# Reordering three ScalarE steps and two VectorE steps in the first two token pairs of a four-layer conditional residual kernel

## The chip, the cores and the metric

The kernel runs on one core of a Trainium2 chip. The metric is the device time of one execution in microseconds; the number given for a kernel is the median of its runs. A profile is one further execution, recorded by the hardware profiler. The core's engines are called PE (TensorE), ACT (ScalarE), DVE (VectorE), POOL (GpSimd) and SP (SyncE, which issues most transfers here). PSUM is the memory that PE writes, SBUF the one from which all engines read.

## The reference

Four residual layers are applied one after the other to x (32 sequences of 64 tokens, 1024 features), all in float32:

```
x = x + W0[adapter[b]] applied across the 64 tokens of sequence b
x = x + x @ W1 + (x @ A1[adapter[b]]) @ B1[adapter[b]]
x = x + x @ W2.T + 0.5 * (x @ A2[labeler[b]]) @ B2.T
logits = x @ Wr.T + 5.0 * onehot(language[b]);   top 2 of 8, softmax -> gates
x = x + x @ W3.T + 2 * sum over experts e of gates[e] * (x @ A3[e].T) @ B3[e].T
```

## The kernel before

**Folding.** The three wide layers are linear up to the low-rank terms, so the kernel multiplies the weight matrices (I + W1)(I + W2)(I + W3) into one 1024 x 1024 matrix first; this takes about the first 245 us of the profile. Then it runs over the tokens, 128 (two sequences, a "block") at a time. Two blocks make a pair; there are eight pairs.

**Two-part numbers.** Every matmul operand is kept as a high part (ACT or POOL writes it, rounded) and a low part (the value minus the high part, mostly on DVE). A product takes three matmuls: high x high, low x high, high x low. Making the two parts of an operand is called splitting it: `..._hi` on ACT, `..._lo` on DVE.

**Seven products.** The product of a pair of blocks with the folded matrix is a Strassen-Winograd product of 2 x 2 quarters: seven products p1 to p7 in place of eight, with sums of the left quarters (made on POOL, in `first_sum` and `pair_sums`) and four combinations t1 to t4 of the right quarters b11, b12, b21 and b22. The combinations are formed once, on DVE (`front_sum`, `back_sum`), and split once (`combination_hi` on ACT, `split_lo` on DVE). Each has a front of three rows of blocks, 128 x 1536 elements in memory, and a back of one row, 128 x 512. The first pair (`first_pair_products`) uses the plain eight quarter products, so that the combinations are needed only from the second pair on, where the calls `there("t1")` to `there("t4")` in `pair_products(1, ...)` wait for the low parts.

**A block's chain.** `narrow` multiplies the block with the 232 narrow columns (low-rank matrices, router). `xn_hi` and `xn_lo` split the result, `mixed` applies the layer-0 matrix. DVE copies the first low-rank activations to `h1c` (`first_low_rank`), PE transposes them (`h1_across`), ACT copies the transpose to `h1T` (`h1_t`), PE multiplies (`h1_into`). The same follows for the second layer with `h2c` (`second_low_rank`), `h2_across`, `h2T` (`h2_t`) and `h2_into`. Then come `route` (the top 2), `exp_of` on ACT, `gates` (which ends in `gh`), and `gated_across`, PE's transpose of `gh`. Then four output tiles are multiplied (`tile`). PE's order has these small steps written in by hand between parts of the wide products.

**What sets the order.** Each engine executes one list of instructions, written out by hand, with semaphore waits; an instruction that waits holds up everything behind it on its engine. The first pair has its own lists (`first_pair_hi` on ACT, `first_pair_lo` on DVE). The second pair is `pair_hi(1, ...)` and `pair_lo(1, ..., after_first=True)`, whose extra lines split t2 and t4. The third-layer low-rank matrix b3 is loaded by SP (line 555) and split on ACT and DVE; it is needed for the first output tile.

In the second pair b0 is block 2 and b1 is block 3. In the rows, line 1165 is the one helper for every `..._lo`, line 1365 is `back_sum`, line 1370 `front_sum`, line 1077 b3's split on ACT, line 879 the ACT copy of a back row, line 1028 `h2_t`, line 1004 the split of a left operand, line 1036 `exp_of`, line 1548 the last step of `gates`, line 1566 `sum_p7`, lines 1510 and 1515 `second_low_rank`. On PE line 1932 is a wide product of the first pair, line 1869 one of the other pairs, line 1896 `h2_across`, line 1901 `h2_into`, line 1885 `h1_across`, line 1906 `gated_across`. On POOL line 697 is `first_sum`, line 681 the last left sum of a row pair of the folding stage, line 643 the low part of the layer-0 matrix.

Of the kernel before, what the change touches and what calls it, by code (L numbers as in the profile page):

```python
# [35 lines left out]
def cond_resid_kernel(nc, x, idx_adapter, idx_labeler, idx_language, w0, w1, a1, w2, a2, b2, w3, b3, out):  # L36
# [59 lines left out]
    def at(name, shape, dtype, offset):  # L96
        return nc.alloc_sbuf_tensor_at(name, shape, dtype, offset=offset)

    def pair(name, shape, offset):
        size = 4  # L100
        for n in shape[1:]:
# [31 lines left out]
                  t4=[W2S[z][:, 0:KQ, BANK:BANK + F3C] for z in range(2)])  # L133
# [35 lines left out]
    def low_back(name):  # L169
# [5 lines left out]
              t3=at("t3_hi", [P, KH, BANK], F32R, X0 + 5 * HALF), t4=M12[0])  # L175
# [94 lines left out]
    with ExitStack() as ctx:  # L270
# [126 lines left out]
        FRONT, BACK = "f", "b"  # L397
# [347 lines left out]
        def _(act):  # L745
# [127 lines left out]
            def split_hi(name, part):  # L873

                dst = m_operand(name, 0) if name[0] == "b" else TH[name]
                if part == FRONT:
                    nc.scalar.activation(dst[:, 0:KF, :], raw_front(name), ACT.Copy).then_inc(s_mh, 1)
                else:
                    nc.scalar.activation(dst[:, KF, :], raw_back(name), ACT.Copy).then_inc(s_mh, 1)

            def combination_hi(name, part):
                act.wait_ge(s_tf if part == FRONT else s_tb, FORMED[name])
                split_hi(name, part)

            def plain_hi(dst, src):
                nc.scalar.activation(dst, src, ACT.Copy).then_inc(s_ph, 1)
# [27 lines left out]
            def row_out(j, name, src):  # L914
                nc.scalar.activation(m_row(j, name), src[:, :], ACT.Copy).then_inc(s_ra, 1)
# [100 lines left out]
            def xn_hi(b, to):  # L1016

                act.wait_ge(s_nar, b + 1)
                above(act, s_small, 3 * b - 2)
                nc.scalar.activation(XN[0], quarters(bank[to][:, 0:SC]), ACT.Copy).then_inc(s_xnh, 1)  # L1020

            def h1_t(b, s):
                act.wait_ge(s_th, 2 * b + 1)
                nc.scalar.activation(h1T[s][:, :], bank[RT + s][0:2 * SEG1, Z1], ACT.Copy).then_inc(s_hts, 1)

            def h2_t(b, s):
                act.wait_ge(s_th, 2 * b + 2)
                nc.scalar.activation(h2T[s][:, :], bank[RT + s][0:SEG2, Z2], ACT.Copy).then_inc(s_hts, 1)
# [9 lines left out]
            def xm_hi(slot, src):  # L1038
                nc.scalar.activation(XM[slot][0], src[:, :], ACT.Copy).then_inc(s_xmh, 1)
# [13 lines left out]
            def first_pair_hi():  # L1053

                for j in range(NR):
                    rows_pair_hi(j)
                act.wait_ge(s_radd, 3 * (NR - 1))
                split_hi("b22", FRONT)
                act.wait_ge(s_ra, 2 * NR)
                split_hi("b12", BACK)  # L1060
                act.wait_ge(s_rw, PRODUCTS * NR)
                row_out(LASTR, "b21", bank[BB])
                act.wait_ge(s_ra, 2 * NR + 1)
                split_hi("b21", BACK)
                act.wait_ge(s_radd, 3 * NR)
                split_hi("b22", BACK)
                act.wait_ge(s_raw[1], 16 * (NR + 2))
                plain_hi(CS[0], raw[1][:, 0:KH, :])
                plain_hi(DS[0], raw[1][:, KH:K, :])
                combination_hi("t3", FRONT)  # L1070
                combination_hi("t1", FRONT)
                combination_hi("t1", BACK)
                xn_hi(0, YB)
                combination_hi("t2", FRONT)
                h1_t(0, 0)
                act.wait_ge(s_b3, 16)
                nc.scalar.activation(B3[0][:, :], b3raw[:, :], ACT.Copy).then_inc(s_b3h, 1)
                combination_hi("t3", BACK)
                h2_t(0, 0)
                left_hi(1)  # L1080
                exp_of(0)
                combination_hi("t2", BACK)
                xn_hi(1, YB)
                act.wait_ge(s_nar, 2)
                act.wait_ge(s_pw, 3)
                xm_hi(0, bank[BA])
                h1_t(1, 1)
                xm_hi(1, bank[BB])
                ght_hi(0, 0)
                h2_t(1, 1)  # L1090
                combination_hi("t4", FRONT)
                combination_hi("t4", BACK)
                exp_of(1)
                xn_hi(2, YB + 1)
                act.wait_ge(s_pw, 5)
                act.wait_ge(s_mix, 1)
                xm_hi(0, bank[BD_])
                ost_even(0, 0)
                ght_hi(1, 1)
                act.wait_ge(s_mix, 2)  # L1100
                xm_hi(1, bank[BC])
                first_ost_odd(1)
                ost_even(0, 2)
                first_ost_odd(3)
# [56 lines left out]
        def _(dve):  # L1161
# [214 lines left out]
            def split_lo(name, part):  # L1376

                dst = m_operand(name, 0) if name[0] == "b" else TH[name]
                dve.wait_ge(s_mh, SPLIT_HI[name + part])
                if part == FRONT:  # L1380
                    out_ = m_operand(name, 1)[:, 0:KF, :] if name[0] == "b" else low_front(name)
                    lo(out_, raw_front(name), dst[:, 0:KF, :], s_ml)
                else:
                    out_ = m_operand(name, 1)[:, KF, :] if name[0] == "b" else low_back(name)
                    lo(out_, raw_back(name), dst[:, KF, :], s_ml)
# [88 lines left out]
            def ght_lo(b, s):  # L1474
                dve.wait_ge(s_ghh, b + 1)
                lo(GHT[s][1][:, :], bank[RT + s][:, Z1], GHT[s][0][:, :], s_ghl)
# [16 lines left out]
            def first_low_rank(b, s, steps):  # L1493
                nar = bank[RT + s]
                dve.wait_ge(s_small, 3 * b + 1)
                for h in range(PER):
                    ts, at_ = slice(h * T, (h + 1) * T), C3 + PER * R2 + h * R1
                    steps.then(V.tensor_copy(h1c[ts, h * SEG1:h * SEG1 + 2 * R1].rearrange("p (m r) -> p m r", m=2),
                                             nar[ts, at_:at_ + R1].unsqueeze(1).to_broadcast([T, 2, R1])))
                steps.hold()  # L1500
                for h in range(PER):
                    ts, at_ = slice(h * T, (h + 1) * T), C3 + PER * R2 + h * R1
                    lo(h1c[ts, h * SEG1 + 2 * R1:(h + 1) * SEG1], nar[ts, at_:at_ + R1], h1c[ts, h * SEG1:h * SEG1 + R1], s_h1c)
# [122 lines left out]
            def pair_lo(p, last, steps, after_first=False):  # L1626
                b0, b1 = 2 * p, 2 * p + 1
                ops = OPS * p - OPS

                operand_lo(CS[1], tmp[:, :, :], CS[0], ops + 2)  # L1630
                first_low_rank(b0, 0, steps)
                if after_first:
                    dve.wait_ge(s_tf, FORMED["t4"])
                    split_lo("t2", FRONT)
                    dve.wait_ge(s_tb, FORMED["t4"])
                    split_lo("t2", BACK)
                operand_lo(DS[1], tmp[:, :, :], DS[0], ops + 3)
                second_low_rank(b0, 0, steps)
                operand_lo(XB[1][:, :, :], raw[1][:, :, :], XB[0][:, :, :], ops + 4)
                route(b0, 0, steps)  # L1640
                if after_first:
                    split_lo("t4", FRONT)
                    split_lo("t4", BACK)
                    xn_lo(b1, YB)
                sum_p1(p)
                operand_lo(CS[1], raw[1][:, 0:KH, :], CS[0], ops + 5)
                sum_p5(p)
                if not after_first:
                    xn_lo(b1, YB)
                gates(b0, 0, steps)  # L1650
                operand_lo(XB[1][:, 0:KH, :], tmp[:, :, :], XB[0][:, 0:KH, :], ops + 6)
                first_low_rank(b1, 1, steps)
                ght_lo(b0, 0)
                sum_p7(p)
                second_low_rank(b1, 1, steps)
                xm_lo(0, bank[BA], 4 * p + 1)
                if not last:
                    left_lo(p + 1)
                route(b1, 1, steps)
                xm_lo(1, bank[BD_], 4 * p + 2)  # L1660
                gates(b1, 1, steps)
                if not last:
                    xn_lo(b0 + 2, YB + 1)
                ght_lo(b1, 1)
                xm_lo(0, bank[BC], 4 * p + 3)
                xm_lo(1, bank[BB], 4 * p + 4)
                ost_odd(p, 1)
                ost_odd(p, 3)
# [467 lines left out]
```

## Time and profile before

| what | value |
|---|---|
| time, median of 3 runs | 523.62 us (523.47 to 523.71) |
| the profiled execution | 525.11 us, of which the span is 523.1 us |
| PE busy | 515.4 us (99%) |
| PEld (weight load, overlaps PE) busy | 449.3 us (86%) |
| DVE busy | 333.1 us (64%) |
| ACT busy | 201.1 us (38%) |
| POOL busy | 169.2 us (32%) |
| granted TensorE clock | full in all of the span |

The span is the time from the first to the last recorded instruction; the rest of the profiled execution lies around it. Busy time counts instructions that run, not those that wait. Times in rows are microseconds from the start of the span.

### The profile page before, as it was taken

The numbers are of one execution on the slowest core, as the hardware profiler recorded it, in microseconds if no ns is written. First come the engines' busy times: TensorE is split into PE (matmuls) and PEld (weight loads), VectorE is DVE, ScalarE is ACT, GpSimd is POOL, SyncE is SP. The second block draws the span as 40 slices with busy tenths as digits, with TensorE's granted clock in tenths as the row PEclk, the third lists the DMA queues.
The fourth block names the chain that finished last, engine by engine and source line by source line (L and its number), as shares of the span: only waits on it lengthen the run. The fifth ranks groups of instructions, "written<-read, shape, count | busy, mean of one in ns | idle before, by whom it ended". The sixth has DMA issues, their size and how long they took to land.

```text
span 523.1 us, 8849 instructions
## 1 busy us (share of the span) xinstructions
PE 515.4 (99%) x2716; PEld 449.3 (86%) x2716; DVE 333.1 (64%) x654; ACT 201.1 (38%) x349; POOL 169.2 (32%) x250
## 2 busy tenths in 40 slices
PE   7999999999999999999999999999999999999997
PEld 7999999988988888888788788888888888888885
DVE  3798797699533333399776864756647557476464
ACT  5644652345132222267344333323332333333322
POOL 2540000002102020219546434444254434553400
PEclk9999999999999999999999999999999999999999
DMA  8911310213430202040703303313233032222312
GB/s 262 375 60 27 72 40 1 80 41 122 154 116 0 81 0 81 0 166 3 241 1 117 121 12 123 104 41 113 83 115 120 37 113 85 75 84 77 125 28 80
DMA packets 29343, 46.80 MB, mean 89 GB/s; under 512 B 12020, under 2 KB 17396, under 8 KB 29188
## 3 DMA queue, kind: packets, MB, share of 16 engines
q1 hardware_dynamic: 29124, 45.85, 26.8%
q0 software_dynamic: 192, 0.59, 0.3%
q8 instruction: 16, 0.26, 0.2%
q14 instruction: 11, 0.09, 0.1%
HBM read 33.39 MB, written 13.04 MB: 89 GB/s over the span
## 4 chain that ended last, share of the span: by engine, by line
PE 91%; DMA 2%; POOL 1%; issue 1%; SPq 1%; DVE 1%; POOLq 1%; ACT 1%; ACTq 0%; DVEq 0%
PE bank L1869 25%; PE bank L1803 13%; PE bank L1735 11%; PE bank L1858 8%; PE bank L1777 6%; PE bank L1789 5%; PE bank L1706 4%; PE bank L1917 4%; PE bank L1925 4%; PE bank L1690 3%; PE bank L1932 2%; PE bank L1920 1%; DMA b3raw<-in_b_dram 1%; PE bank L1919 1%; DMA w2raw<-in_w_dram 1%
## 5 line engine op out<-in xcount | busy, mean ns | idle before, releaser
L1869 PE MATMUL bank<-t_hi,em_hi 128*128 128x512 f32 x168 | 57.5, 403 | 0.0
L1165 DVE TENSOR_TENSOR w1t_lo<-raw,w1t_hi 128x1024 fp32r<-128x1024 f32 x18 | 24.5, 1362 | 23.3 <-ACT w1t_hi L897 17.1
L672 POOL TENSOR_TENSOR tmp<-raw 128x512 f32<-128x512 f32 x4 | 7.2, 1794 | 97.0 <-DVE raw L1351 97.0
L1869 PEld LDWEIGHTS bank<-t_hi,em_hi 128*128 128x128 f32 x168 | 31.2, 189 | 7.2 <-DVE em_hi L1165 0.4
L1803 PE MATMUL bank<-te,em_hi 128*128 128x512 f32 x144 | 34.9, 395 | 0.0
L658 POOL CAST em_hi<-tba 128x256 fp32r x32 | 13.3, 446 | 63.6 <-PE bank L1858 60.0
L1803 PEld LDWEIGHTS bank<-te,em_hi 128*128 128x128 f32 x144 | 27.0, 188 | 6.5
L1165 DVE TENSOR_TENSOR em_hi<-tmp,em_hi 128x512 fp32r<-128x512 f32 x22 | 15.1, 686 | 21.7 <-ACT em_hi L1004 12.6
L662 POOL TENSOR_TENSOR em_lo<-tba,em_hi 128x256 fp32r<-128x256 f32 x32 | 27.4, 876 | 2.4 <-POOL em_hi L658 1.2
L1735 PE MATMUL bank<-em_hi,w2s_hi 128*128 128x384 f32 x80 | 27.0, 337 | 0.0
L1735 PE MATMUL bank<-em_lo,w2s_hi 128*128 128x384 f32 x80 | 27.0, 337 | 0.0
L1735 PE MATMUL bank<-em_hi,w2s_lo 128*128 128x384 f32 x80 | 26.9, 337 | 0.0
L1165 DVE TENSOR_TENSOR em_lo<-bank,em_hi 128x232 fp32r<-128x232 f32 (+2 forms) x36 | 16.7, 484 | 14.5 <-ACT em_hi L1020 11.2
L1869 PE MATMUL bank<-ml,em_hi 128*128 128x512 f32 x63 | 25.5, 405 | 0.0
L1165 DVE TENSOR_TENSOR w2s_lo<-w2raw,w2s_hi 128x768 fp32r<-128x768 f32 (+4 forms) x15 | 20.3, 1362 | 6.2 <-ACT w2s_hi L773 3.3
L1869 PE MATMUL bank<-em_hi,w1t_lo 128*128 128x512 f32 x56 | 22.6, 404 | 0.0
L1869 PE MATMUL bank<-em_hi,w1t_hi 128*128 128x512 f32 x56 | 22.2, 396 | 0.0
L1869 PE MATMUL bank<-em_lo,w1t_hi 128*128 128x512 f32 x56 | 22.2, 396 | 0.0
L1706 PE MATMUL bank<-g,w2s_hi 128*128 128x392 f32 x96 | 18.8, 343 | 1.6 <-ACT w2s_hi L773 1.6
L1789 PE MATMUL bank<-em_lo,w1t_hi 128*128 128x296 f32 x64 | 19.2, 301 | 0.0
L662 POOL TENSOR_TENSOR em_lo<-a1raw,em_hi 128x128 fp32r<-128x128 f32 x32 | 19.2, 619 | 0.0
L1789 PE MATMUL bank<-em_hi,w1t_lo 128*128 128x296 f32 x64 | 19.1, 298 | 0.0
(293 smaller groups left out, 1609.0 us busy)
## 6 DMA issues: line engine op xcount, KB each, us to landing
raw<-in_x_dram SPq DMA_DIRECT2D x16, 512.0 KB, 4.0
b1s<-b1scr SPq DMA_DIRECT2D x32, 217.5 KB, 2.7
raw<-in_b1w_dram SPq DMA_DIRECT2D x10, 512.0 KB, 3.2
out_dram<-ef SPq DMA_DIRECT2D x16, 256.0 KB, 2.0
out_dram<-ost SPq DMA_DIRECT2D x16, 256.0 KB, 2.3
graw<-in_w3a3wr_dram SPq DMA_DIRECT2D x4, 768.0 KB, 11.0
b1scr<-b1stage SPq DMA_DIRECT2D x12, 256.0 KB
w2raw<-in_w_dram SPq DMA_DIRECT2D x7, 384.0 KB, 6.8
```

The source lines that it names most:

```text
L662: nc.gpsimd.tensor_tensor(S[1][:, :, at_:at_ + n], src, f32(S[0][:, :, at_:at_ + n]), ALU.subtract).then_inc(s_sel, 1)
L1165: V.tensor_tensor(dst, src, f32(hi), ALU.subtract).then_inc(signal, 1)
L1690: ins = nc.tensor.matmul(to[:, 0:w], lhs, G[c][z][:, k, 0:w], start=(k == 0 and n == 0), stop=(k == K - 1 and n == len(terms) - 1), skip_g ...
L1706: ins = nc.tensor.matmul(bank[ob][:, 0:WIDTH_A[c]], W2S[a][:, k, ob * P:(ob + 1) * P], G[c][z][:, k, 0:WIDTH_A[c]], start=(k == 0 and (a, ...
L1735: ins = nc.tensor.matmul(to[j][:, 0:F3C], left[a][:, k, j * P:(j + 1) * P], G_RIGHT[name][z][:, k, :], start=(opens and n == 0), stop=(n = ...
L1777: ins = nc.tensor.matmul(stage_bank(r, j)[:, 0:cols.stop - cols.start], W1T[r][a][:, k, :], EM[z][:, k, cols], start=(k == 0 and (a, z) == ...
L1789: ins = nc.tensor.matmul(bank[RT + h][:, 0:EC], left[a][:, k, :], EM[z][:, k, EXT], start=(k == 0 and (a, z) == TERMS[0]), stop=(k == K - ...
L1803: ins = nc.tensor.matmul(to[:, :], left[a][:, k0 + k, :], e_right(right, z, k), start=(name in OPENS and n == 0), stop=(n == 3 * KH - 1), ...
L1858: ins = nc.tensor.matmul(bank[to][:, 0:SC], left(a, k), S[z][:, k, :], start=(k == 0 and (a, z) == TERMS[0]), stop=(k == K - 1 and (a, z) ...
L1869: ins = nc.tensor.matmul(to[:, :], left[a][:, k0 + k, :], m_right(right, z, k), start=(name in OPENS and n == 0), stop=(n == 3 * KH - 1), ...
L1917: ins = nc.tensor.matmul(to[:, :], BD[s][a][:, :], XM[n % 2][z], start=(a, z) == TERMS[0], stop=False, skip_group_check=True)
L1925: ins = nc.tensor.matmul(to[:, :], GHT[s][a][:, :], B3[z][:, cols], start=False, stop=(a, z) == TERMS[-1], skip_group_check=True)
```

## The change

On ACT, in the first pair, the split of b3's high part moves behind two steps that stood behind it: the high part of t3's back row and `h2_t(0, 0)`. On DVE, in the second pair, the two low parts of t4 move from behind `route(b0)` to behind `first_low_rank(b1)`. No instruction is added or removed, and no wait is changed; each wait moves with its instruction.

```diff
                 xn_hi(0, YB)
                 combination_hi("t2", FRONT)
                 h1_t(0, 0)
+                combination_hi("t3", BACK)
+                h2_t(0, 0)
                 act.wait_ge(s_b3, 16)
                 nc.scalar.activation(B3[0][:, :], b3raw[:, :], ACT.Copy).then_inc(s_b3h, 1)
-                combination_hi("t3", BACK)
-                h2_t(0, 0)
                 left_hi(1)
                 exp_of(0)
...
                 route(b0, 0, steps)
                 if after_first:
-                    split_lo("t4", FRONT)
-                    split_lo("t4", BACK)
                     xn_lo(b1, YB)
                 sum_p1(p)
...
                 gates(b0, 0, steps)
                 operand_lo(XB[1][:, 0:KH, :], tmp[:, :, :], XB[0][:, 0:KH, :], ops + 6)
                 first_low_rank(b1, 1, steps)
+                if after_first:
+                    split_lo("t4", FRONT)
+                    split_lo("t4", BACK)
                 ght_lo(b0, 0)
                 sum_p7(p)
```

## Rows read from the trace of the kernel before

**Rows 1.** The page's first line: the span.
```profile
span 523.1 us, 8849 instructions
```

**Rows 2.** Waits of PE in the whole span: total us, times, longest us.
```profile
PE bank L1901 <- ACT h2T L1028: 0.6, 1, 0.6
PE bank L1906 <- DVE gh L1548: 0.6, 1, 0.6
```

**Rows 3.** Timeline of PE, first pair: start us, duration us, instruction [idle before <- releaser].
```profile
256.93 0.27 PE L1896 MATMUL bank<-ident,h2c 128*128 128x128 f32 x1
...
258.19 0.40 PE L1932 MATMUL bank<-em_lo,em_hi 128*128 128x512 f32 x1
258.43 0.40 PE L1932 MATMUL bank<-em_hi 128*128 128x512 f32 x1
259.43 0.30 PE L1901 MATMUL bank<-b2s,h2T 128*128 128x136 f32 x1 [0.61 <-ACT h2T L1028]
```

**Rows 4.** Timeline of ACT, first pair.
```profile
257.55 1.06 ACT L1077 ACTIVATE b_hi<-b3raw 128x1024 fp32r<-128x1024 f32 x1 [3.53 <-DMA b3raw<-in_b_dram]
258.51 0.61 ACT L879 ACTIVATE t_hi<-ef 128x512 fp32r<-128x512 f32 x1
259.03 0.26 ACT L1028 ACTIVATE h2T<-bank 128x128 fp32r<-128x128 f32 x1
260.08 1.06 ACT L1004 ACTIVATE w1t_hi<-raw 128x1024 fp32r<-128x1024 f32 x1 [0.79 <-DMA raw<-in_x_dram]
261.05 0.28 ACT L1036 ACTIVATE ex<-top 128x1 f32<-128x1 f32 x1
```

**Rows 5.** Timeline of DVE, first pair: t3's back row is formed.
```profile
256.12 0.69 DVE L1365 TENSOR_TENSOR ef<-ef 128x512 f32<-128x512 f32 x1
```

**Rows 6.** Timeline of DVE, second pair.
```profile
291.80 1.75 DVE L1165 TENSOR_TENSOR ml<-mr,m_hi 128x1536 fp32r<-128x1536 f32 x1
293.47 0.68 DVE L1165 TENSOR_TENSOR em_lo<-ef,m_hi 128x512 fp32r<-128x512 f32 x1
294.59 0.40 DVE L1165 TENSOR_TENSOR em_lo<-bank,em_hi 128x232 fp32r<-128x232 f32 x1 [0.43 <-ACT em_hi L1020]
...
298.57 0.29 DVE L1548 TENSOR_TENSOR gh<-bank,gate 128x128 f32<-128x128 f32 x1
...
300.22 0.29 DVE L1165 TENSOR_TENSOR ght_lo<-bank,ght_hi 128x128 fp32r<-128x128 f32 x1
301.30 0.70 DVE L1566 TENSOR_TENSOR bank<-bank,held_p 128x512 f32<-128x512 f32 x1 [0.78 <-PE bank L1869]
...
302.47 0.41 DVE L1515 SCALAR_TENSOR_TENSOR h2c<-bank,h2c 64x32 fp32r<-64x32 f32 x2
```

**Rows 7.** Timeline of PE, second pair.
```profile
298.92 0.33 PE L1906 MATMUL bank<-ident,gh 128*128 128x128 f32 x1 [0.56 <-DVE gh L1548]
...
303.06 0.27 PE L1896 MATMUL bank<-ident,h2c 128*128 128x128 f32 x1
```

**Rows 8.** Timelines of DVE and POOL where both read SBUF, and POOL's sum in the second pair.
```profile
224.51 1.29 POOL L681 TENSOR_TENSOR raw<-raw,raw 128x512 f32<-128x512 f32 x1 [2.58 <-DVE w1t_lo L1165]
224.59 2.83 DVE L1165 TENSOR_TENSOR em_lo<-mr,em_hi 128x1536 fp32r<-128x1536 f32 x1 [0.15 <-ACT em_hi L877]
...
246.53 1.76 DVE L1370 TENSOR_TENSOR mr<-mr 128x1536 f32<-128x1536 f32 x1
246.65 1.96 POOL L643 TENSOR_TENSOR bd_lo<-ef,bd_hi 128x128 fp32r<-128x128 f32 x1
248.20 1.82 DVE L1165 TENSOR_TENSOR em_hi<-raw,em_hi 128x512 fp32r<-128x512 f32 x2
...
301.13 1.29 POOL L697 TENSOR_TENSOR tmp<-raw 128x512 f32<-128x512 f32 x1 [2.82 <-DMA raw<-in_x_dram]
```

**Rows 9.** The transfers into the raw tile, all of the span.
```profile
DMA to landing us min/median/max: 3.0/3.9/5.9
```

## The prediction

> **What bounds the kernel now.** I read the page first. Its span [rows 1] is 523.1 us, and the profiled execution took 525.11 us in all: 2.01 us lie around the span. The three plain runs have a median of 523.62 us. I make every sum against the span and put the difference on that median. A difference within 0.2% (1.05 us) is about what a measurement of this kernel can't tell from no change.
>
> Next I asked who waits for whom on TensorE. In the whole execution only two waits of PE behind another engine's work in the late part are named [rows 2]: one for `h2T` and one for `gh`. Otherwise TensorE goes from matmul to matmul. So an idle stretch of PE that goes away shortens the span by its length, and one that arises lengthens it by its length; nothing later has slack to swallow it. The change touches two places: one around 257 us, in the first token pair, and one from 291 to 303 us, in the second pair. I read the timelines of PE, ScalarE (ACT), VectorE (DVE) and GpSimd (POOL) there, one engine at a time.
>
> **Part 1, ScalarE's order.** The transpose that feeds `h2T` starts on PE at 256.93 [rows 3]. The copy that makes `h2T` starts only at 259.03 [rows 4], because it stands third in a queue: ACT is idle 3.53 us until b3's transfer lands, splits b3 (1.06 us), makes t3's back row (0.61 us), and then comes to `h2T`. On PE two 512-column matmuls in a row start 0.24 us apart (258.19 and 258.43), so the matmul with `h2T` was due at 258.43 + 0.24 = 258.67. It started at 259.43. That is 0.76 us lost.
>
> With the new order: t3's back row is formed on DVE by 256.12 + 0.69 = 256.81 [rows 5], so its ACT copy can start at about 256.86. The next ACT instruction behind such a copy starts 0.52 us later (258.51 to 259.03 [rows 4]), so `h2T` starts at 257.38; the transpose (256.93 + 0.27 = 257.20 [rows 3]) is done by then. `h2T` is there at 257.38 + 0.26 = 257.64, one microsecond ahead of 258.67. The whole 0.76 us goes.
>
> What does b3's split lose? Its data lands when it starts today, at 257.55, and ACT is free again at about 257.6. So it moves by some 0.05 us. Behind it on ACT stands the split of the next left block, which waits for its own transfer until 260.08 [rows 4]; b3's split now ends near 258.7, still 1.4 us before. No transfer is issued by ACT, and no wait is added: the waits move with their instructions. If the transfer of b3 were later, the new order would keep PE out of it, so the cost here is nothing from below; the bound above is the 0.05 us. What is late next: `exp_of(0)` stays at 261.05 (it is behind the 260.08 transfer), so DVE's gates can start at 261.05 + 0.28 = 261.33 at the earliest. They feed `gh` of block 0, and PE has no wait for that one today [rows 2]. Everything from there to the second pair is released by PE and moves up with it. **Part 1: -0.76 us.** In what follows I keep the old clock, and shift at the end.
>
> **Part 2, VectorE's order.** Today t4's split stands between route(b0) and `xn_lo(b1)`: front 291.80 for 1.75 us, back 293.47 for 0.68 us [rows 6], over at 294.15. Then DVE is idle 0.43 us, until ACT has the high part of block b1's narrow result. So `xn_lo(b1)` at 294.59 is not held by the split: taken away, the split leaves a hole. `xn_lo(b1)`, the sums, the gates and `gh` (298.57) keep their times, and PE's stall at 298.92 for `gh` [rows 2, 7] stays. Gain in the old place: 0. The bound on that side: the whole `gh` wait of 0.6 us [rows 2] if that order did hold it; I take 0, because of the 0.43 us.
>
> In the new place the two instructions stand behind `first_low_rank(b1)` and ahead of `ght_lo(b0)`, which starts at 300.22 [rows 6]. Queued behind them are `ght_lo`, `sum_p7`, and `second_low_rank(b1)`, whose `h2c` PE transposes at 303.06 [rows 7]. The front takes 293.47 - 291.80 = 1.67 us from start to start. DVE's starts are 0.08 us ahead of the end before them (291.80 + 1.75 = 293.55 against 293.47), so the back takes 0.60. `ght_lo` goes to 300.22 + 2.27 = 302.49 and `sum_p7` to 302.49 + 0.29 - 0.08 = 302.70. Today `sum_p7` starts at 301.30, having waited 0.78 us for PE. So of the 2.27 us, 0.87 us are hidden, and 1.40 us are late. `h2c` is ready at 302.47 + 0.41 = 302.88 today, and at 304.28 then. From the end of the DVE instruction to PE's transpose it takes 0.06 us (298.57 + 0.29 = 298.86, and 298.92 [rows 6, 7]), so PE starts it at 304.34 instead of 303.06: **a new stall of 1.28 us.** Behind it `h2_t(b1)`, the split of pair 2's left block, and DVE's work on it are released in turn and are late by the same amount, with no second charge. p4 needs t4's low part only after that transpose, at which point it has long been there.
>
> Then the neighbour on GpSimd. POOL's sum for pair 2 starts at 301.13, for 1.29 us [rows 8]: in the middle of the new slot of t4's front (300.22 to 301.97). It doesn't touch what DVE does there today, which reads PSUM. t4's split reads two operands in SBUF, as do the rows that show a clash: the same 128x1536 instruction took 2.83 us beside a POOL sum (224.51 and 224.59), against 1.75 us alone, so 1.08 us more. There POOL started first. Where DVE starts first, POOL waits and then takes its turn: `bd_lo`, of 128x128, recorded from 246.65 to 248.61, ends 0.32 us behind DVE's 248.29; and DVE's next two subtractions (248.20) take 1.82 us for the 0.68 + 0.60 = 1.28 of two such alone [rows 8]. So I expect POOL's sum to run between t4's front and its back, and the back to end some 1.08 us later. The bounds are 0 (POOL comes behind both, or after they are done) and 1.29 (its whole length); I take 1.08, the row of the same pair of instructions. The stall grows to 1.28 + 1.08 = 2.36 us.
>
> The Trainium skill bears on this place (SBUF — State Buffer, section Who interferes with whom): a DVE instruction with two SBUF inputs and a GpSimd instruction that reads SBUF exclude each other for a whole instruction, and issue order decides who blocks. The 2.83 us row agrees in kind. By that rule the charge would be the full 1.29 us and the total 0.21 us larger than by the row. It speaks against this change, as the new place is beside a POOL sum and the old one is not.
>
> **Sum.** -0.76 + 1.28 + 1.08 = **+1.60 us**: the span goes to 524.7 us, the median to 523.62 + 1.60 = 525.2 us, 0.31% slower.
>
> **Rivals.**
> *A, the clash on SBUF happens:* +1.60 us, 525.2 us. For it: POOL's start at 301.13 lies 0.91 us behind the beginning and 0.84 us ahead of the end of t4's front. If its transfer lands earlier, POOL goes first and the front waits instead. Chance 0.64.
> *B, no clash:* -0.76 + 1.28 = +0.52 us, 524.1 us, within 0.2%. It needs POOL's sum to start after 301.97, that is, its transfer to land 0.84 us later, or DVE to win the turn. Transfers of this kind landed in 3.0 to 5.9 us [rows 9]. Chance 0.18.
> *C, part 1 gives nothing:* another wait takes its place, or the gain is lost before the second pair: +1.28 + 1.08 = +2.36 us, 526.0 us. Against it: `h2T` has 1.0 us to spare, and no other wait of PE is named in between. Chance 0.07.
> *D, the other side, faster:* t4's split does hold DVE's chain to `gh`, and the new place is covered. Then the wait at 298.92 (0.6 us [rows 2]) goes too: -0.76 - 0.6 = -1.4 us, 522.3 us. It decides from the point at which the split would end later than 294.59, where `xn_lo(b1)` starts, and it ends at 294.15; and the new place would need 2.27 us of idle DVE where there are 0.78. Chance 0.05.
> *E, only part 1 shows:* the split fits behind PE's work: -0.76 us, 522.9 us, within 0.2%. Against it: the same 0.78 us. Chance 0.06.
>
> **Numbers.** The likeliest is A, 525.2 us. The range is to hold B (524.1), A with its clash of up to 1.29 us (525.4), and C (526.0): 523.9 to 526.0 us. Slower by over 0.2% (above 524.67): A and C, 0.71, less a little for an A with a short clash: 0.70. Within 0.2%: B, E and that little: 0.25. Faster: D, 0.05.
>
> **What the profile of the changed kernel would show.** Part 1 right: ACT makes t3's back row and `h2T` before b3's split, near 256.9 and 257.4, the wait for `h2T` is gone from PE's list, and the matmul with it starts near 258.7. Part 2 right: DVE idle for some 2.6 us ahead of `xn_lo(b1)`; PE still waits 0.6 us for `gh`; PE's list has a new wait, for `h2c`, of about 2.4 us on the transpose of block b1 (its start near 304.7 with the shift; 303.6 without the clash); POOL's sum longer than 1.29 us in the records and t4's back of about 1.8 us. If the transpose starts near 302.3, part 2 costs nothing and I am wrong about the idle time; if `gh` comes earlier, I am wrong about what holds `xn_lo(b1)`. What would make the size wrong is the turn between DVE and POOL and where the transfer of pair 2's right block lands.

## The result, and the profile after

| kernel | median | executions |
|---|---|---|
| before | 523.62 us | 7, 523.11 to 524.29 |
| after | 526.73 us | 7, 525.60 to 527.58 |

The ratio is 1.0056 (95% interval 1.0046 to 1.0066): slower by 2.9 us by the ratio, where 1.6 us had been forecast. The time lies 0.7 us above the upper end of the range. The seven executions of the changed kernel fall into two groups: three at a mean granted clock of 1.000 took 525.60, 525.63 and 526.19 us, four at 0.997 took 526.73 to 527.58 us. The profiled one is of the first group: 526.19 us, of which the span is 524.1 us. That span is 1.0 us above the one of before [rows 1].

The waits of PE in the changed kernel (total us, times, longest us), against [rows 2]:

```profile
PE bank L1897 <- DVE h2c L1515: 2.3, 1, 2.3
...
PE bank L1907 <- DVE gh L1548: 0.6, 1, 0.6
```

The wait for `h2T` is gone, the wait for `gh` has its old size, and there is a new one for `h2c`. All three are as forecast. PE's line numbers are one higher than before, and b3's split on ACT is now line 1079.

ACT in the first pair of the changed kernel, against [rows 4]:

```profile
256.38 0.63 ACT L879 ACTIVATE t_hi<-ef 128x512 fp32r<-128x512 f32 x1 [2.83 <-DVE ef L1365]
256.91 0.26 ACT L1028 ACTIVATE h2T<-bank 128x128 fp32r<-128x128 f32 x1
257.07 1.05 ACT L1079 ACTIVATE b_hi<-b3raw 128x1024 fp32r<-128x1024 f32 x1
258.82 1.06 ACT L1004 ACTIVATE w1t_hi<-raw 128x1024 fp32r<-128x1024 f32 x1 [0.70 <-DMA raw<-in_x_dram]
```

`h2T` is made ahead of b3's split. But the split no longer waits for anything: in this execution b3's transfer landed 6.4 us after its issue, ahead of 257.07, where the execution of before had 7.4 us. On PE, against [rows 3], the matmul with `h2T` follows the one ahead of it without a gap:

```profile
257.96 0.40 PE L1933 MATMUL bank<-em_hi 128*128 128x512 f32 x1
258.19 0.23 PE L1902 MATMUL bank<-b2s,h2T 128*128 128x136 f32 x1
```

DVE and POOL in the second pair of the changed kernel, against [rows 6, 8]:

```profile
293.28 0.40 DVE L1165 TENSOR_TENSOR em_lo<-bank,em_hi 128x232 fp32r<-128x232 f32 x1 [2.69 <-ACT em_hi L1020]
...
297.28 0.29 DVE L1548 TENSOR_TENSOR gh<-bank,gate 128x128 f32<-128x128 f32 x1
...
298.93 1.76 DVE L1165 TENSOR_TENSOR ml<-mr,m_hi 128x1536 fp32r<-128x1536 f32 x1
300.60 1.78 DVE L1165 TENSOR_TENSOR em_lo<-ef,m_hi 128x512 fp32r<-128x512 f32 x1
302.41 0.29 DVE L1165 TENSOR_TENSOR ght_lo<-bank,ght_hi 128x128 fp32r<-128x128 f32 x1
302.62 0.69 DVE L1566 TENSOR_TENSOR bank<-bank,held_p 128x512 f32<-128x512 f32 x1
...
303.79 0.41 DVE L1515 SCALAR_TENSOR_TENSOR h2c<-bank,h2c 64x32 fp32r<-64x32 f32 x2
```

```profile
300.24 1.60 POOL L697 TENSOR_TENSOR tmp<-raw 128x512 f32<-128x512 f32 x1 [3.23 <-DMA raw<-in_x_dram]
```

The old place of the split is now a hole of 2.69 us, and `gh` stands as far behind `xn_lo(b1)` as it did: 297.28 − 293.28 = 4.00 us, against 298.57 − 294.59 = 3.98. In the new place the front takes its usual 1.76 us. POOL's sum is released at 300.24, in the middle of it, and ends at 301.84, which is 0.31 us more than its 1.29. t4's back stands recorded for 1.78 us instead of 0.68: it waited while POOL had its turn. `sum_p7`, which had waited 0.78 us for PE, now waits for nothing and is late itself.

PE in the second pair of the changed kernel, against [rows 7]:

```profile
297.62 0.33 PE L1907 MATMUL bank<-ident,gh 128*128 128x128 f32 x1 [0.58 <-DVE gh L1548]
...
301.53 0.39 PE L1870 MATMUL bank<-em_lo,xb_hi 128*128 128x512 f32 x1
304.25 0.33 PE L1897 MATMUL bank<-ident,h2c 128*128 128x128 f32 x1 [2.33 <-DVE h2c L1515]
```

The transpose was due 0.23 us behind the matmul of 301.53, at 301.76, and starts 2.49 us late. From `sum_p1` of the second pair to that of the third the trace has 32.37 us before (294.90 to 327.27) and 34.92 us after (293.59 to 328.51): +2.55 us. The spans differ by only 1.0 us, because the changed kernel is ahead when it reaches this place. The matmul ahead of `h2T` starts 0.47 us earlier than before (257.96 against 258.43); nearly all of that arose early, where a stretch of PE's `w2s` products starts at 9.75 us after and 10.18 us before. The matmul with `h2T` starts 1.24 us earlier (258.19 against 259.43). So the two profiles do show part 1 as a gain: 1.24 − 0.47 = 0.77 us. They also hold part 2 at about the size that was forecast (+2.36 us). What they don't show is whether the 0.77 us is there in other executions, and why four executions in seven took longer still.

### The profile page after: what moved, and what is told of

It is laid out like the page before. It is cut to its first block, busy times and chain, and to the rows that moved or that the text cites. A ratio compares the mean times of both kernels' runs of the same rounds, so it can differ in the third digit from the quotient of the medians.

```text
span 524.1 us, 8849 instructions
## 1 busy us (share of the span) xinstructions
PE 515.8 (98%) x2716; PEld 449.8 (86%) x2716; DVE 333.9 (64%) x654; ACT 201.3 (38%) x349; POOL 168.3 (32%) x250
## 4 chain that ended last, share of the span: by engine, by line
PE 95%; DVE 2%; DMA 1%; SPq 0%; issue 0%; ACT 0%; POOL 0%; ACTq 0%; DVEq 0%
PE bank L1870 25%; PE bank L1804 15%; PE bank L1736 11%; PE bank L1859 8%; PE bank L1778 6%; PE bank L1790 5%; PE bank L1707 4%; PE bank L1918 4%; PE bank L1933 4%; PE bank L1926 4%; PE bank L1691 3%; PE bank L1921 1%; PE bank L1920 1%; DMA w2raw<-in_w_dram 1%; PE bank L1880 1%; PE bank L1897 0%
```

## The experiments

The runs were made in four groups; within a group they share a chip and the runs of the kernel before: e1 to e4 (before 523.82 us), e5 to e8 (523.99 us), e9 and e10 (523.65 us), e11 and e12 (524.17 us). The last column counts the executions at a mean granted clock of 0.997 or less. The kernel before has none among its 83 executions in these groups. A mean of 0.999, which some executions have, is no such case: in the profiles with it (e6, e7, e9, e11, e12) the clock is below 1.00 only behind PE's last matmul.

| run | median, us | ratio to before (95%) | low clock |
|---|---|---|---|
| e1 part 1 alone | 523.49 | 0.9993 (0.9984 to 1.0002) | 0 of 11 |
| e2 part 2 alone | 527.52 | 1.0065 (1.0052 to 1.0077) | 3 of 6 |
| e3 the change again | 526.18 | 1.0045 (1.0032 to 1.0058) | 0 of 5 |
| e4 POOL's sum later | 524.93 | 1.0025 (1.0014 to 1.0035) | 0 of 8 |
| e5 a longer stall | 530.15 | 1.0110 (1.0086 to 1.0135) | 4 of 4 |
| e6 only t4's back moved | 523.71 | 0.9992 (0.9983 to 1.0001) | 0 of 11 |
| e7 b3 late, old order | 526.90 | 1.0056 (1.0039 to 1.0073) | 4 of 8 |
| e8 b3 late, new order | 524.25 | 1.0007 (0.9995 to 1.0020) | 0 of 10 |
| e9 splits and gates moved | 524.16 | 1.0006 (0.9997 to 1.0015) | 0 of 11 |
| e10 splits alone moved | 525.08 | 1.0026 (1.0014 to 1.0037) | 0 of 7 |
| e11 the change, gates earlier | 523.63 | 0.9993 (0.9984 to 1.0002) | 0 of 11 |
| e12 back moved, gates earlier | 523.37 | 0.9982 (0.9973 to 0.9991) | 0 of 11 |

### e1 and e2: each part alone

e1 has the ACT edit of the change alone, e2 the DVE edit alone.

> Only ScalarE's order is changed: t3's back row and h2_t(0, 0) ahead of b3's split. Theory S (the profile's sum: part 1 takes out 0.76 us of TensorE's waiting and nothing else): the time is 0.8 us below before, near 522.9 us, and the wait for h2T is gone. Rival T (part 1 itself carries the 1.5 us that the whole change lost beyond my sum): the time is above before, by about 0.7 us.

> Only VectorE's order is changed: t4's two low parts behind first_low_rank(b1). Theory S: 1.28 + 1.08 = 2.36 us above before, near 526.0 us, with a wait for h2c of 2.3 us. Rival U (the new stall of 2.3 us makes TensorE slower after it, by a lower granted clock in a part of the executions): 3.5 to 4.5 us above before, and executions that show a mean granted clock below 1.000.

e1 gained 0.33 us by the medians, less than half of the 0.76 us. Its interval, from a gain of 0.84 us to a loss of 0.10 us, holds 0.76 us too, so the times alone don't decide; rival T, a loss, they exclude. e2 lost 3.7 us in the median; its three executions at full clock (526.34, 526.50, 526.86) lost 2.7 us, the three at 0.997 (528.19, 528.19, 528.48) lost 4.4 us. ACT in e2, in the *old* order, shows why part 1 gives less:

```profile
256.11 1.06 ACT L1077 ACTIVATE b_hi<-b3raw 128x1024 fp32r<-128x1024 f32 x1 [2.52 <-DMA b3raw<-in_b_dram]
257.07 0.61 ACT L879 ACTIVATE t_hi<-ef 128x512 fp32r<-128x512 f32 x1
257.59 0.26 ACT L1028 ACTIVATE h2T<-bank 128x128 fp32r<-128x128 f32 x1
```

b3 landed 6.4 us after its issue there, `h2T` was in time, and PE's list of waits has no `h2T`. With a landing of 7.4 us PE lost 0.76 us [rows 3, 4], so the loss begins at about 7.4 − 0.76 = 6.64 us. In the twelve profiles in which this transfer has its old place it landed after 6.3, 6.4, 6.4, 6.5, 6.7, 6.8, 6.9, 7.0, 7.3, 7.4, 7.6 and 7.8 us. What exceeds 6.64 us comes to 4.4 us over the twelve, 0.37 us each. This estimate agrees with e1's 0.33 us.

The profile of e2 is one at the low clock. Its windows (us, granted clock and busy time of each engine), and PE's timeline in them:

```profile
303.00:304.00 1.00, 0.00 (x0) 0.00 (x0) 0.93 (x4) 0.00 (x0) 0.00 (x0) 1.00 0.00 0
304.00:305.00 1.00, 0.71 (x4) 0.62 (x5) 0.90 (x3) 0.34 (x2) 0.00 (x0) 1.00 0.00 0
305.00:306.00 1.00, 1.00 (x5) 0.77 (x4) 0.07 (x1) 1.00 (x2) 0.00 (x0) 0.59 0.06 16
306.00:307.00 1.00, 1.00 (x4) 0.86 (x3) 1.00 (x1) 0.39 (x1) 0.00 (x0) 0.50 0.00 0
307.00:308.00 1.00, 1.00 (x4) 0.76 (x3) 0.76 (x7) 0.30 (x1) 0.00 (x0) 0.50 0.00 0
308.00:309.00 1.00, 1.00 (x5) 0.83 (x4) 0.93 (x5) 0.00 (x0) 0.00 (x0) 0.70 0.00 0
309.00:310.00 1.00, 1.00 (x7) 0.82 (x6) 0.89 (x5) 0.00 (x0) 0.00 (x0) 1.00 0.00 0
```

```profile
304.29 0.33 PE L1897 MATMUL bank<-ident,h2c 128*128 128x128 f32 x1 [2.32 <-DVE h2c L1515]
...
304.70 0.40 PE L1870 MATMUL bank<-em_hi,xb_hi 128*128 128x512 f32 x1
304.93 0.40 PE L1870 MATMUL bank<-em_lo,xb_hi 128*128 128x512 f32 x1
...
307.05 0.63 PE L1870 MATMUL bank<-m_hi,xb_hi 128*128 128x512 f32 x1
307.47 0.63 PE L1870 MATMUL bank<-ml,xb_hi 128*128 128x512 f32 x1
```

The last number but two in a window is the granted clock. PE waits 2.32 us and goes on at full speed, its matmuls 0.23 us apart. About a microsecond later the clock falls to 0.50, the lower of its two levels (1.2 GHz), the matmuls stand 0.42 us apart, and the clock is back at 1.00 before 309. The four windows miss 0.41 + 0.50 + 0.50 + 0.30 = 1.71 us of full-speed work, and 1.71 of 526.4 us is a mean clock of 0.997: the value that the slower executions carry. It is also their extra time: 528.19 − 526.50 = 1.69 us. The profile of the changed kernel, with the same wait (2.33 us), has 1.00 in all these windows, and so has that of e3 (2.34 us).

### e3: the change once more

> The changed kernel once more, to see whether the loss of 3.1 us (526.73 against 523.62) comes again beside the two halves on one chip. Theory S gives 1.6 us above before. Rival U gives 2 us above before in the executions whose mean clock is 1.000 and 3 to 4 us in those at 0.997. If the loss is a matter of the chip of that measurement, it is nearer 1.6 us here.

Five executions, all at full clock: 525.77 to 526.76 us, 2.36 us above before. The 526.73 us of the result and these 526.18 us are one kernel; they differ in how many executions had the low clock. Over the changed kernel, e2 and e3, all with a wait of 2.3 us, it came in 4 + 3 + 0 = 7 of 18.

### e4: POOL's sum behind the second product's sums

```diff
                     pool.wait_ge(s_opl, OPS * p - OPS)
+                    pool.wait_ge(s_add, 3 * p - 3)
```

> The changed kernel, with GpSimd's first_sum(p) held back until VectorE's sum_p7 of the pair before is done (one wait more on GpSimd), so that it never runs beside t4's split in its new place. Theory S: t4's back takes 0.68 us again, the wait for h2c falls from 2.3 to about 1.3 us, and the time is 1.1 us below the changed kernel's. Rival V (the split's place is what costs, the clash is recorded but hidden): the wait for h2c stays near 2.3 us and the time is the changed kernel's. If rival U holds, the shorter stall may also keep the clock at 1.000, and then the gain is 2 us or more.

DVE, POOL and PE of e4:

```profile
298.73 1.76 DVE L1166 TENSOR_TENSOR ml<-mr,m_hi 128x1536 fp32r<-128x1536 f32 x1
300.40 0.68 DVE L1166 TENSOR_TENSOR em_lo<-ef,m_hi 128x512 fp32r<-128x512 f32 x1
```

```profile
302.09 1.27 POOL L698 TENSOR_TENSOR tmp<-raw 128x512 f32<-128x512 f32 x1 [5.28 <-DVE bank L1567]
```

```profile
302.95 0.33 PE L1898 MATMUL bank<-ident,h2c 128*128 128x128 f32 x1 [1.23 <-DVE h2c L1516]
```

With the sum out of the way the back takes 0.68 us and the wait for `h2c` is 1.23 us, the stall without a clash that the prediction put at 1.28. From pair to pair the trace has 33.81 us, 1.44 above before; e4 − e1 is 1.44 us too, and e3 − e4, the clash, 1.25 us. The stall and the clash are real, and theory S holds; rival V is out. For rival B of the prediction this is its own case: its stall was right, but its time, +0.52 us, was too low, since e4 measured +1.1 us (interval +0.7 to +1.8) with part 1 giving less than 0.76 us. None of the eight executions had the low clock.

### e5: the stall made longer

Behind t4's split ten small fills of `lg`, each waited for, hold DVE for about 1.3 us. `lg` isn't in use at that moment; nothing is left out.

```diff
                     split_lo("t4", BACK)
+                    for n in range(10):
+                        V.memset(lg[:, :], 0.0).then_inc(s_idle, 1)
+                        dve.wait_ge(s_idle, n + 1)
```

> The changed kernel with ten tiny VectorE fills of an unused moment of lg behind t4's split, each waited for, in the second pair alone: they do no work and only lengthen TensorE's wait for h2c, by an estimated 1.5 to 2.5 us (ten of 0.14 us and their waits), from 2.3 to about 4 to 5 us. Rival U (the stall itself brings the clock down behind it, and does so more surely the longer it is): nearly every execution shows a mean clock below 1.000, and the time is above the changed kernel's by the added wait plus about 1.6 us. Rival W (the lower clock has nothing to do with the stall): as many executions as before, about 7 of 18, or none, show it, and the stretch of lower clock need not lie behind the stall.

PE waited 3.6 us, 1.24 us longer than in the changed kernel; expected were 1.5 to 2.5 us more, but the ten fills with their waits took only 1.3 us. All four executions had a low clock: two at 0.997 (528.36 and 529.38 us), two at 0.994 (530.92 and 531.07 us). The windows of e5, profiled at 0.994:

```profile
304.00:305.00 1.00, 0.00 (x0) 0.00 (x0) 0.98 (x3) 0.00 (x0) 0.00 (x0) 0.95 0.00 0
305.00:306.00 1.00, 0.23 (x2) 0.23 (x2) 0.89 (x4) 0.00 (x0) 0.00 (x0) 0.50 0.00 0
306.00:307.00 1.00, 1.00 (x4) 0.81 (x4) 0.44 (x1) 0.72 (x2) 0.00 (x0) 0.50 0.08 16
...
310.00:311.00 1.00, 1.00 (x4) 0.71 (x3) 0.92 (x4) 0.00 (x0) 0.00 (x0) 0.50 0.00 0
311.00:312.00 1.00, 1.00 (x4) 0.80 (x3) 0.91 (x4) 0.00 (x0) 0.00 (x0) 0.63 0.00 0
```

Here the clock falls while PE still stands (its next matmul starts at 305.77), and stays at half until after 311, about twice as long as in e2. Rival U holds and rival W doesn't. That half of the executions lost more than the 1.6 us expected for the clock was not foreseen.

### e6: only t4's back in the new place

Part 1, with `split_lo("t4", FRONT)` left where it was and `split_lo("t4", BACK)` behind `first_low_rank(b1)`.

> Part 1, and of t4's split only the back row (0.68 us, 0.60 from start to start) in the new place; the front stays behind route(b0). Theory S: VectorE has 0.78 us idle ahead of sum_p7, so 0.60 us fit, there is no new wait for h2c beyond 0.1 us, and the time is that of part 1 alone, near 523.5 us. GpSimd's sum starts at 301.13 less the shift, when the back is nearly over (300.22 to 300.90), so there is no clash. Rival V (any split in the new place costs its length): a wait for h2c of 0.6 us or more, 524.1 us.

The back (298.80, 0.69 us) and `ght_lo` (299.52) end before `sum_p7` starts at 299.87, POOL's sum starts behind the back at 300.04, and PE's list has no wait for `h2c`. Its time (523.71 us, a ratio of 0.9992) is that of part 1 alone (0.9993). It confirms the 0.78 us of cover in [rows 6], and that the front is what doesn't fit.

### e7 and e8: b3 loaded later, in the old and the new order

```diff
-            sp.dma_start(b3raw[:, :], b3).then_inc(s_b3, 16)
             sp.wait_ge(s_b1z, 2)
             load_b1s(rows_of(1), 1)
+            sp.dma_start(b3raw[:, :], b3).then_inc(s_b3, 16)
```

> The kernel before, with b3's load issued behind block 1's low-rank rows, some 4.9 us later. Theory X (part 1 is worth what b3's transfer is late: nothing when it lands within about 6.6 us of its issue, 0.76 us in the profile of before with 7.4 us): h2T comes some 5 us later, and TensorE waits 4 to 6 us for it; the time is 4 to 6 us above before, or more where the clock falls. Rival Y (the order on ScalarE hardly matters, since something else releases TensorE there): within 1 us of before.

> The same late load of b3 with ScalarE's new order. Theory X: no wait for h2T at all. What is late next is exp_of(0) and xn_hi of block 1, which stand behind b3's split: TensorE waits about 2 to 3 us for the low part of block 1's narrow result, and the time is 2 to 4 us above before and about 3 us below the old order with the same load. Rival Y: the same time as the old order with the same load.

ACT in e7, in the old order, and then PE:

```profile
259.49 1.06 ACT L1077 ACTIVATE b_hi<-b3raw 128x1024 fp32r<-128x1024 f32 x1 [5.31 <-DMA b3raw<-in_b_dram]
260.45 0.61 ACT L879 ACTIVATE t_hi<-ef 128x512 fp32r<-128x512 f32 x1
260.97 0.26 ACT L1028 ACTIVATE h2T<-bank 128x128 fp32r<-128x128 f32 x1
```

```profile
261.37 0.30 PE L1901 MATMUL bank<-b2s,h2T 128*128 128x136 f32 x1 [2.40 <-ACT h2T L1028]
```

ACT in e8, in the new order:

```profile
257.32 0.26 ACT L1028 ACTIVATE h2T<-bank 128x128 fp32r<-128x128 f32 x1
258.51 1.06 ACT L1079 ACTIVATE b_hi<-b3raw 128x1024 fp32r<-128x1024 f32 x1 [0.93 <-DMA b3raw<-in_b_dram]
```

With b3 later, the old order costs 2.9 us in the median, part of it through the clock (its four executions at full clock lost about 1.8 us), and the new one 0.3 us (interval −0.3 to +1.0). So rival Y is out: ACT's order matters, and the new order keeps PE out of b3's lateness. The sizes expected from theory X were missed, 4 to 6 us and 2 to 4 us above before: issued later, b3 landed faster, after 4.8 us (e7) and 4.0 us (e8), so PE waited 2.4 us in e7 and 0.4 us in e8. The stall of 2.4 us stands in another pair and behind another engine than that of the changed kernel, and half of the executions (4 of 8) had the low clock. None of these four was profiled, so where their clock fell isn't shown.

### e9 and e10: is there a place that is covered?

Both have part 1 and form t2's low parts at the end of the first pair, t4's low parts in t2's old place. e9 also moves the gates of block b0 ahead of `xn_lo(b1)`:

```diff
                 if after_first:
+                    gates(b0, 0, steps)
                     xn_lo(b1, YB)
...
                 if not after_first:
                     xn_lo(b1, YB)
-                gates(b0, 0, steps)
+                    gates(b0, 0, steps)
```

> A version made from the profile: ScalarE's new order (part 1); t2's low parts move into VectorE's idle 3.2 us at the end of the first pair; t4's take the place that t2's had, behind first_low_rank(b0); and gates(b0) moves ahead of xn_lo(b1), into the hole of 2.7 us that t4's split leaves there. Theory S: TensorE's wait of 0.6 us for gh and the 0.23 us for h1c in the second pair are gone, no wait for h2c arises, and the time is 0.7 to 1.0 us below part 1 alone, near 522.6 us. Rival Z (gates ahead of the sums makes sum_p5 or the split of the left sum late, so the wait only moves to p7): within 0.3 us of part 1.

> The same without moving gates(b0): it stays behind sum_p5. Theory S: xn_lo(b1) is not held by any split, so the wait for gh stays at 0.6 us and the time is that of part 1, 523.5 to 523.7 us (at best 0.2 us less, since t2's split no longer stands ahead of the second left sum's). Rival D of the prediction (t4's split held the chain to gh): the wait for gh is gone and the time is 0.7 us or more below part 1.

Neither was faster, and both expectations were missed: e9 was to reach 522.6 us and e10 523.5 to 523.7 us. In the new places DVE met POOL again. DVE and POOL of e9:

```profile
283.82 1.93 DVE L1165 TENSOR_TENSOR ml<-mr,m_hi 128x1536 fp32r<-128x1536 f32 x1
285.67 1.78 DVE L1165 TENSOR_TENSOR em_lo<-ef,m_hi 128x512 fp32r<-128x512 f32 x1
```

```profile
284.09 2.81 POOL L731 TENSOR_TENSOR tmp<-tmp,raw 128x512 f32<-128x512 f32 x1
```

PE then waited 0.9 us for the low part behind it, in e9 and in e10, which took what was won. The two runs differ by 0.92 us in the gates alone: the wait of 0.6 us for `gh` is in e10 and not in e9. So the gates did hold PE, and the hole ahead of `xn_lo(b1)` is the place to make them.

### e11 and e12: gates in the hole

e11 is the changed kernel with the gates moved as in e9; e12 is e6 with them between t4's front and `xn_lo(b1)`.

> The changed kernel with one step more moved, in the second pair alone: gates(b0) ahead of xn_lo(b1), in the hole that t4's split left. Theory S (gates moved are worth 0.9 us, e9 against e10; t4's split of 2.27 us in its new place now begins near 298.1 on the clock of before and ends near 300.4, ahead of GpSimd's sum at 301.1, so there is no clash): no wait for gh, a wait for h2c of at most 0.3 us, and 0.5 to 0.9 us below part 1 alone: 522.6 to 523.1 us. Rival Z (the split collides again, with GpSimd's low parts of the next narrow columns or with the sum): a wait for h2c of 1 us or more, and no less than part 1.

> Part 1, t4's back row in the new place, its front in the old one, and gates(b0) between the front and xn_lo(b1). Theory S: gates push xn_lo(b1) back by about 0.4 us and the second left sum's split with it, which then stands behind GpSimd's first low part: the wait for gh goes, but one of 0.2 to 0.7 us for sum_p5 or xn_lo comes; 523.0 to 523.6 us. Rival Z': everything fits, 522.8 us.

DVE of e12:

```profile
290.69 1.75 DVE L1165 TENSOR_TENSOR ml<-mr,m_hi 128x1536 fp32r<-128x1536 f32 x1
...
293.98 0.29 DVE L1548 TENSOR_TENSOR gh<-bank,gate 128x128 f32<-128x128 f32 x1
294.19 0.39 DVE L1165 TENSOR_TENSOR em_lo<-bank,em_hi 128x232 fp32r<-128x232 f32 x1
...
297.80 0.69 DVE L1165 TENSOR_TENSOR em_lo<-ef,m_hi 128x512 fp32r<-128x512 f32 x1
298.53 0.29 DVE L1165 TENSOR_TENSOR ght_lo<-bank,ght_hi 128x128 fp32r<-128x128 f32 x1
299.86 0.70 DVE L1566 TENSOR_TENSOR bank<-bank,held_p 128x512 f32<-128x512 f32 x1 [1.03 <-PE bank L1871]
```

e11 takes back the whole loss of the change: the later work on DVE starts earlier, the wait for `h2c` shrinks to 0.6 us and that for `gh` is gone. But it is no faster than part 1 alone (0.9993 both), which theory S had asked for: t4's two low parts still ran beside POOL's `em_lo` (line 662) and took 1.87 and 0.95 us. e12 has neither of the two waits, but one of 0.2 us for a low part, as expected, and is the one version clear of before: 523.37 us, 0.8 us faster (interval 0.5 to 1.4 us). Its interval overlaps those of e1 and e11, so that it beats part 1 alone isn't shown.

## Why the prediction was right about the sign and wrong about the size

**Part 2, +1.28 and +1.08 us: right.** Forecast were a hole, an unchanged wait for `gh`, `h2c` late by 1.28 us without the clash and 2.36 us with it, and a back of about 1.8 us. The traces show a hole of 2.69 us, 0.6 us, recorded waits of 1.23 us (e4) and 2.33 us, and a back of 1.78 us. Counted as the prediction counted, by the start of the transpose against `sum_p1`, it is late by 1.39 us (e4) and 2.50 us. POOL took its turn between front and back, as argued. The term taken from the row of the same pair of instructions (1.08 us) measured 1.78 − 0.68 = 1.10 us. The rule of the Trainium skill (SBUF — State Buffer, section Who interferes with whom), by which the blocked side stands for the other's whole instruction, would have given 1.29 us; it holds in kind here, and for the size the measured 1.10 us decides. In the times, part 2 beside part 1 (e3 − e1) is 2.69 us, 0.3 us more than forecast, and the clash (e3 − e4) 1.25 us, which is too rough to tell 1.10 from 1.29.

**Part 1, −0.76 us: the mechanism was right, the term mis-sized.** The step that failed is "The whole 0.76 us goes". `h2T` did come in time, and against that one profile of before the gain is 0.77 us. But the 0.76 us were those of one execution in which b3 landed after 7.4 us. The median over executions gained 0.33 us (e1), in line with 0.37 us estimated from twelve landings. The profiled execution of before was itself late, 525.11 us against a median of 523.62. The prediction never asked why; the 0.77 us and the 0.47 us from ahead of it (both against the changed kernel's profile) come near these 1.49 us. So the term was probably subtracted from a median that had only a part of it.

**"So an idle stretch of PE ... one that arises lengthens it by its length": failed.** This is the step behind the range. In 11 of 18 executions a stall of 2.3 us cost about its length (2.7 us in e2 against before, and in e3 against e1), and in 7 of 18 some 1.7 us more, by the granted clock, which in e2's profile is at half for 3.4 us. No term stood for it, and no rival. With the two corrections the sum is: 523.62 − 0.33 + 2.36 = 525.65 us at full clock (measured 525.60, 525.63, 526.19), and with 1.7 us more 527.35 us (measured 526.73 to 527.58). Four of seven executions were of the second kind, so the median fell among them. How many there are is, as far as the runs show, luck: with none, as in e3, the change costs 2.36 us, which from 523.62 us is 526.0 us, the upper end of the range. That the stall is the cause, and not a neighbour on the chip, rests on the counts: 0 of 8 behind 1.2 us (e4), 7 of 18 behind 2.3 us, 4 of 8 behind 2.4 us (e7), 4 of 4 behind 3.6 us (e5), and 0 of 72 in e1, e6 and e8 to e12, whose longest wait of PE behind another engine in the token pairs is 0.9 us; and 0 of 83 in the kernel before beside them, on the same chips.

**Rivals.** A's mechanism is what happened, with part 1 smaller and the clock's share on top. B was made true by e4, and its stall was right. C (526.0 us) lies near the median for another reason: part 1 did give something. E is out with the new stall. D is refuted: the split did not hold `gh`, since in the changed kernel and in e10, with the split gone from there, the wait of 0.6 us stayed. What holds it is the order of the gates behind `xn_lo(b1)` (e9 against e10), which the prediction didn't ask.

**What stays open.** e3 − e1 is 0.3 us above the recorded wait of 2.34 us. Of these, 0.2 us are in the trace: from pair to pair e3 has 34.91 us, 2.54 above before. The rest is within the noise. e3 had no low clock in five executions, where the same kernel had four in seven. If 7 low ones fall at random among 18, a given five are all clear in about 1 case of 19, so chance is possible; no run tells more. Nor does any run show what decides whether the clock falls behind a stall of 2.3 us.

## What to carry to other kernels

Before two instructions are moved, look at what the neighbour engine does in the new place; here 1.1 of 2.4 us came from POOL's turn, and moving only the part that fits (e6) cost nothing. A stall is priced by its length only while it is short: near 2.3 us it cost a further 1.7 us in part of the executions, through the clock, so forecast two times with shares and not one. Both numbers are of this kernel; where between 1.2 and 2.3 us of waiting it begins wasn't measured. And a wait that ends on a transfer must be read in more than one execution before it is booked as a gain.

## What the runs showed of the hardware

**The clock.** After a wait of 2.3 us PE ran on for a microsecond at full speed before the granted clock fell to 0.50, so the loss stands behind the stall and not in it (e2, the one profile of this kind); with 3.6 us it fell during the wait (e5). The Trainium skill (TensorE: Matmul & The Clock Gate, Part 1: The HAM clock gate) says that recent activity decides between two levels, and that executions of one kernel differ in how many matmuls run at the lower one at its start. The levels agree with the 1.00 and 0.50 of these windows. That the changed kernel can go either way in its middle (4 of 7) is of the same kind, but no run here shows that it has the same reason.

**One transfer, many landings.** The same 512 KB transfer of b3, issued at 249.5 to 250.1 us in twelve profiles, landed after 6.3 to 7.8 us; issued about 5 us later, at 254.7 and 254.4 us, after 4.8 and 4.0 us (e7, e8).
